# Projecting the third attention's keys straight into the layout of its scores

## The reference, cut to what matters

```python
x = x + _L0_xattn_ref(_layernorm(x), ctx, ...)   # 16 heads of 8, biases, clip
x = x + _L0_ffn_ref(_layernorm(x), ...)          # 8 experts, top 2, gelu
x = x + _L1_xattn_ref(_layernorm(x), ctx, ...)   # 16 heads of 64
x = x + _L1_ffn_ref(_layernorm(x), ...)          # one float8 GEMM, 128 x 128
x = x + _L2_xattn_ref(_layernorm(x), ctx, ctx, ...)  # 16 heads of 8, biases
x = x + _L2_ffn_ref(_layernorm(x), ...)          # 8 experts, relu
x = x + _L3_xattn_ref(...); x = x + _L3_ffn_ref(...)
...
q = (query @ Wq + bq).reshape(B, Nq, 16, 8).transpose(0, 2, 1, 3)   # L2_xattn
k = (key @ Wk + bk).reshape(B, Nk, 16, 8).transpose(0, 2, 1, 3)
v = (value @ Wv + bv).reshape(B, Nk, 16, 8).transpose(0, 2, 1, 3)
attn = softmax(einsum('bhqd,bhkd->bhqk', q, k) * 8 ** -0.5)
return einsum('bhqk,bhkd->bhqd', attn, v).transpose(0, 2, 1, 3).reshape(B, Nq, 128) @ Wo + bo
```

## Time and profile before

| | |
|---|---|
| median of 3 runs | 3913.32 us (3908.84 to 3914.06) |
| the profiled execution, its own time | 3909.72 us |
| its span, first to last instruction | 3908.0 us |
| mean granted TensorE clock | 0.978 |
| PE / ACT / DVE / POOL busy | 93 / 66 / 44 / 12 % |
| DMA, moved | 183.19 MB, mean 47 GB/s |

### The profile page before, as it was taken

One profiled execution on the slowest core, in us unless ns is written; L12 is line 12 of the kernel. 1 busy time (PEld: TensorE's weight loads), 2 busy tenths in 40 slices (PEclk: granted clock), 3 DMA queues, 4 the chain that ended last, 5 costly groups with the idle time before them and its releaser, 6 DMA issues.

```text
span 3908.0 us, 84669 instructions
## 1 busy us (share of the span) xinstructions
PE 3636.0 (93%) x31202; PEld 1368.8 (35%) x31202; DVE 1722.0 (44%) x1678; ACT 2583.1 (66%) x2749; POOL 459.1 (12%) x1842
## 2 busy tenths in 40 slices
PE   7999999999899999999999999968888889897989
PEld 4333333335433333333333333421111123453444
DVE  4222222223377777777777777730000011344344
ACT  5999999983355556555555555469999999401321
POOL 1222222220000000000000000012222222001210
PEclk8999999998999999999999999989999999998989
DMA  5323232212111111111111110050101000000000
GB/s 174 102 76 105 82 100 81 95 70 70 53 32 43 39 38 39 37 39 43 39 37 39 37 37 1 17 149 4 38 4 38 4 29 1 17 27 0 0 13 28
DMA packets 109881, 183.19 MB, mean 47 GB/s; under 512 B 23700, under 2 KB 46896, under 8 KB 107408
## 3 DMA queue, kind: packets, MB, share of 16 engines
q1 hardware_dynamic: 109584, 178.75, 14.9%
HBM read 107.13 MB, written 71.57 MB: 46 GB/s over the span
## 4 chain that ended last, share of the span: by engine, by line
PE 71%; ACT 12%; issue 11%; DVE 4%; ACTq 1%; DMA 0%; SPq 0%; POOL 0%; POOLq 0%; DVEq 0%
PE ps L725 18%; PE ps L750 18%; ACT probs L1050 12%; PE ps L503 7%; PE ps L489 4%; PE ps L437 3%; PE ps L629 3%; PE ps L608 2%; PE ps L866 2%; PE ps L877 2%; PE ps L442 2%; PE ps L925 2%; PE ps L939 1%; PE ps L615 1%; PE ps L262 1%
## 5 line engine op out<-in xcount | busy, mean ns | idle before, releaser
L1050 ACT ACTIVATE probs<-ps 128x1024 f32<-128x1024 f32 x1632 | 1512.8, 1081 | 58.9 <-PE ps L489 58.7
L1149 ACT ACTIVATE probs<-ps 128x1024 f32<-128x1024 f32 x816 | 836.1, 1025 | 596.0 <-PE ps L725 583.1
L1813 DVE TENSOR_TENSOR vbuf<-vbuf,probs 128x1024 f32<-128x1024 f32 (+1 forms) x800 | 972.8, 1224 | 334.7 <-ACT probs L1149 334.7
L503 PE MATMUL ps<-probs,vst 128*32 128x512 f32 x6528 | 863.0, 600 | 118.0 <-ACT probs L1050 117.4
L489 PE MATMUL ps<-qz,kst 32*128 32x512 f32 x3264 | 414.7, 495 | 25.1 <-issue 17.3
L489 PEld LDWEIGHTS ps<-qz,kst 32*128 32x128 f32 x3264 | 162.3, 182 | 710.4 <-issue 682.5
L1302 POOL CAST kst<-kb 128x128 fp32r x816 | 244.8, 300 | 1283.1 <-PE ps L503 1172.5
L1627 DVE COPY qs<-ps 128x512 f32<-128x512 f32 (+1 forms) x208 | 141.7, 681 | 576.0 <-PE ps L437 283.0
L725 PE MATMUL ps<-probs,kb 64*64 64x512 f32 x2560 | 332.2, 589 | 0.0
L725 PE MATMUL ps<-probs,qz 64*64 64x512 f32 x2048 | 269.8, 594 | 7.1 <-issue 6.9
L750 PE MATMUL ps<-probs,qz 64*64 64x512 f32 x2048 | 266.8, 590 | 0.0
(11 more groups left out here) (365 smaller groups left out, 3073.8 us busy)
## 6 DMA issues: line engine op xcount, KB each, us to landing
kv_scratch<-qs SPq DMA_DIRECT2D x192, 256.0 KB, 2.0
kb<-k_scratch SPq DMA_DIRECT2D x24, 816.0 KB, 7.4
kb<-kv_scratch SPq DMA_DIRECT2D x72, 256.0 KB, 2.9
qz<-kv_scratch SPq DMA_DIRECT2D x64, 256.0 KB, 2.9
k_scratch<-klo SPq DMA_DIRECT2D x24, 512.0 KB, 3.5
vbuf<-in_L_ffn_W SPq DMA_DIRECT2D x32, 256.0 KB, 3.1
klo<-kv_scratch SPq DMA_DIRECT2D x32, 256.0 KB, 2.9
qs<-kv_scratch SPq DMA_DIRECT2D x24, 256.0 KB, 2.9
```

The costliest lines, as they stand in the source:

```text
L503: mm = pe.matmul(ps[32 * j:32 * j + 32, 6 + half, :], vst[:, r, 32 * j:32 * j + 32], probs[:, r, j * HT:(j + 1) * HT], start=start, stop=stop)
L1050: act.activation(probs[:, r, b * T:(b + 1) * T].rearrange("p (h n) -> p h n", h=2), ps[:, 2 * buf:2 * buf + 2, :], ACT.Exp, scale=HD8 ** - ...
L1149: act.activation(pr1[:, (u + 2 * odd) % 4], ps[:, 2 * b:2 * b + 2, :], ACT.Exp, scale=HD64 ** -0.5)\
L1813: dve.tensor_tensor(sum1[0:k, odd, h], sum1[0:k, odd, h], e, ALU.add).then_inc(s["added"], 1)
```

## The change

1. **Layer 2's keys never go through DRAM.** `spread_weights` repeats each column of the key weights four times (`w64`) and of the first group's query weights (`wqs`), so a projection lands in the layout of the scores. DVE makes high and low parts with two per-lane factors (`lane`). Chunk 0 of group 0 is made ahead of the attention; the other 12 key chunks, ten of the 13 value chunks and the second half of group 0's queries become 23 jobs (`FIRST2`), done as two half jobs each in tiles 0 to 45 of half 0, all through PSUM bank 7. The keys of the next group are projected in halves 1, 3 and 5, 13 chunks each at `V3_AT`'s tiles, through bank 6. SP loads only queries.
2. **Preparation of layer 2.** Per chunk only a key projection and a square from PSUM remain (`keys2`); the largest norm is taken once per four chunks, each chunk's 128-column blocks lying on four groups of 32 partitions. No sum is taken. The order of PE, ACT and DVE is written out.
3. **Layer 0's norms** also go to four row blocks, with largest value and sum once per four chunks; then a spreading matmul and three small DVE steps pick each head's largest value.
4. **float8:** the layernorm writes bfloat16 directly (the cast goes), and the overflow test masks the sign off where it squared; its four steps (`tensor_tensor`, two `tensor_scalar`, `tensor_tensor`) become three `tensor_scalar`s.
5. `sums1` of the last pair comes after the output projection's first pair; ACT no longer waits for `comb_ready` before `experts8(0)`, and `best` works in another buffer for 8 experts. One small DMA (`bqs`) is added.

```diff
+FIRST2 = [("k", 1), ("k", 2), ("k", 3)]
+FIRST2 += [job for c in range(VEARLY, NC) for job in (("v", c), ("k", c + 1)) if job[1] < NC]
+FIRST2 += [("q", 0)]
...
+                def keys_spread(g, c, p0, p1, bank):
+                    c0, wd = CHUNKS[c]
+                    p1 = min(p1, wd)
+                    for j in range(G):
+                        cut = slice(32 * j, 32 * j + 32)
+                        mm = pe.matmul(ps[cut, bank, p0:p1], w64[:, g, cut], ctxT[:, c0 + p0:c0 + p1], start=True, stop=True)
+                    if p1 == wd:
+                        mm.then_inc(s["k_proj"], 1)
+                def first_job(k, p0, p1):
+                    kind, c = FIRST2[k]
+                    if p0 == 0:
+                        before_kind, before_c = FIRST2[k - 1] if k else ("k", 0)
+                        if before_kind == "k":
+                            pe.wait_ge(s["k_split"], NC + before_c + 1)
+                        else:
+                            pe.wait_ge(s["v_copied"], CHUNKED[2] + before_c + 1)
...
+                            elif gh == 0:
+                                if t < 2 * len(FIRST2):
+                                    first_job(t // 2, t % 2 * (HT // 2), (t % 2 + 1) * (HT // 2))
+                            elif half and g + 1 < NG:
+                                for k in range(V3_PARTS):
+                                    if V3_AT[k] == t:
+                                        next_keys(gh, k // 2, k % 2 * (HT // 2), (k % 2 + 1) * (HT // 2))
...
-            sums1(last_pair, 1, 1)
...
             for p in range(NP):
+                if p == 1:
+                    sums1(last_pair, 1, 1)
...
-            keys8(1, 2, {0: lambda: ln_mean(3), 1: lambda: ln_var(3), 2: lambda: ln_spread(3), 4: float8,
-                         5: lambda: ln_mean(4), 6: lambda: ln_var(4), 7: lambda: ln_spread(4),
-                         9: lambda: queries8(1, 2, 4), 11: lambda: query_norms8(1)})
+            keys2(0)
+            pe.wait_ge(s["x_ready"], 4)
+            ln_mean(3)
+            keys2(1)
+            key_norms(1, 0)
+            ln_var(3)
+            keys2(2)
+            key_norms(1, 1)
+            ln_spread(3)
+            for c in range(3, 9):
+                keys2(c)
+                key_norms(1, c - 1)
+            float8()
...
+            ln_mean(4)
+            keys2(11)
+            key_norms(1, 10)
+            ln_var(4)
+            keys2(12)
+            key_norms(1, 11)
+            ln_spread(4)
+            key_norms(1, 12)
+            pe.matmul(ps[:, 7, :], w64[:, 0, :], ctxT[:, 0:HT], start=True, stop=True).then_inc(s["k_proj"], 1)
+            queries8(1, 4)
+            key_norms_spread(1)
+            pe.matmul(ps[:, 3, :], wqs, z[:, 0, :], start=True, stop=True).then_inc(s["q_proj"], 1)
+            query_norms8(1)
+            values8(1, 2, 0)
+            values8(1, 2, 1)
+            spread_bound2()
+            values8(1, 2, 2)
             attention8(1, 2)
...
-            act.wait_ge(s["comb_ready"], 1)
             experts8(0)
...
+                def next_keys(g, c, bank):
+                    c0, wd = CHUNKS[c]
+                    dve.wait_ge(s["k_proj"], 2 * NC + g * NC + c + 1)
+                    then(dve.tensor_scalar(klo[:, 0, 0:wd].bitcast(F32R), ps[:, bank, 0:wd], lane[:, 1:2], None, ALU.mult))
+                    dve.scalar_tensor_tensor(out=kb[:, g % 2, c0:c0 + wd], in0=ps[:, bank, 0:wd], scalar=lane[:, 0:1],
+                                             in1=klo[:, 0, 0:wd], op0=ALU.mult, op1=ALU.add).then_inc(s["k_split"], 1)
+                def other_queries():
+                    halves = qs[:, :, :].rearrange("p l (h n) -> p l h n", h=2)
+                    dve.wait_ge(s["k_high"], NC + 3)
+                    then(dve.tensor_copy(halves[:, 0].bitcast(F32R), t1))
+                    dve.tensor_tensor(halves[:, 1].bitcast(F32R), t1, halves[:, 0], ALU.subtract).then_inc(s["q_split"], 1)
...
-                then(dve.tensor_tensor(b, a, a, ALU.mult))
-                then(dve.tensor_scalar(b, b, FP8_MAX ** 2, 3e38, ALU.is_gt, ALU.mult))
-                then(dve.tensor_scalar(b, b, 3e38, None, ALU.mult))
-                then(dve.tensor_tensor(b, b, b, ALU.subtract))
+                then(dve.tensor_scalar(b.bitcast(I32), a.bitcast(I32), 0x7FFFFFFF, None, ALU.bitwise_and))
+                then(dve.tensor_scalar(b, b, FP8_MAX, 3e38, ALU.is_gt, ALU.mult))
+                then(dve.tensor_scalar(b, b, 3e38, 0.0, ALU.mult, ALU.mult))
```

More of the change, by code:

```diff
@@ new lines, in key_norms @@
+            def key_norms(n, c):
+                bank, at = norm_place(n, c)
+                pe.wait_ge(s["norm_sq"], n * NC + c + 1)
+                if n == 0 and c and c % 4 == 0:
+                    pe.wait_ge(s["norm_max"], c // 4)
+                for j in range(CHUNKS[c][1] // P):
+                    mm = pe.matmul(ps[32 * j:32 * j + 32, bank, at:at + P], heads[:, :], t3b[:, c % 2, j * P:(j + 1) * P],
+                                   start=True, stop=True)
+                if c % 4 == 3 or c + 1 == NC:
+                    mm.then_inc(s["norm_mm"], 1)
@@ new lines, in key_norms_spread, with values8 @@
+            def key_norms_spread(n):
+                pe.wait_ge(s["norm_max"], n * (KGROUPS + 1) + KGROUPS + 1)
+                pe.matmul(ps[:, 2, 0:P], peak[:, kmax].to_broadcast([P, P]), ident[:, :], start=True, stop=True)\
+                    .then_inc(s["norm_mm"], 1)
+            def values8(n, layer, c):
+                t0, m = VG[c]
+                if c >= 2:
+                    pe.wait_ge(s["v_copied"], CHUNKED[layer] + c - 1)
+                for u in range(m):
+                    mm = pe.matmul(ps[:, 4 + c % 2, u * P:(u + 1) * P], ctxT[:, (t0 + u) * P:(t0 + u + 1) * P],
+                                   w8[:, n, 2, :], start=True, stop=True)
+                mm.then_inc(s["v_proj"], 1)
@@ L393, in keys8 @@
                         .then_inc(s["k_proj"], 1)
-                    t0, m = VG[c]
-                    if c >= 2:
-                        pe.wait_ge(s["v_copied"], CHUNKED[layer] + c - 1)
-                    for u in range(m):
-                        mm = pe.matmul(ps[:, 4 + c % 2, u * P:(u + 1) * P], ctxT[:, (t0 + u) * P:(t0 + u + 1) * P],
-                                       w[:, 2, :], start=True, stop=True)
-                    mm.then_inc(s["v_proj"], 1)
+                    values8(0, 0, c)
@@ L515, in qk_maxima @@
                             return mm
+                        if n and g * 2 + half == 0:
+                            for k in range(len(FIRST2)):
+                                first_job(k, 0, HT)
                         maxima(layer, g * 2 + half, G, 2 * ST, qk_maxima)
@@ L533, in group @@
                             stream(first, lambda t, r: qk(half, t, r), lambda *at: av(g, half, *at), last_sums)
+                            if half and g + 1 < NG:
+                                for c in range(NC):
+                                    next_keys(g * 2 + half, c, 0, HT)
                             if g * 2 + half == CENTRED:
@@ L1248, in _ @@
             diagonal(picks[:, :], [[-1, E16]], 0)
[L1249 removed]
+            for j in range(1, G):
+                diagonal(picks[:, :], [[-1, E16]], -32 * j)
             const(pool.memset(ctxT[C:P, ONES:S], 1.0))
@@ L1648, in without_jobs8 @@
                 def without_jobs8(gi, par, half, p):
+                    if p == 0:
+                        for k in range(len(FIRST2)):
+                            first_job(k)
+                            if k == 0:
+                                other_queries()
+                        dve.wait_ge(s["q_split"], 6)
                     with dve.If(mode >= 1):
```

476 lines of the change are left out of this document (315 added, 161 removed).

## The result

The changed kernel takes 6837.45 us (median of 4 runs, 6832.1 to 6841.72), the kernel before 3911.8 beside it: a ratio of 1.748, 95% interval 1.745 to 1.751. It is 2926 us slower where 22.7 us faster were forecast. Its profiled execution has a span of 6838.0.

The account below looks back on a forecast made before the run. PE's queue was taken as the chain, with ACT's exponentials setting plain tiles and nothing covering layer 2's preparation. Terms -30 + 6.7 + 2.7 - 3.3 + 1.0 + 0.2 = -22.7 gave 3888 us, range 3875 to 3902.

Parts of the forecast that it names:

- fourth layernorm to the register: Layer 2's preparation, from the float8 matmul's result to the bound in the register: 33.9 us becomes 16, gain 17.9, 1.0 given back.
- uncovered jobs: Rival: 124 half jobs in layer 2's halves 0, 1, 3, 5 each add 0.43 us of PE work; 3929 us, chance 0.04.
- PE's wait: Between layer 2's register and PE's first scores: 7.2 us becomes 4.3 with idle DMA engines, gain 2.9, or 0.
- Halves 1 to 6: Layer 2's key jobs in halves 1, 3 and 5 cost 0.90 us each, +2.7 in all; bounds 0 and +8.
- half 7 is the row: Layer 2's old half 7, with 26 half jobs, took 0.90 us over a plain half; taken as price for halves 1, 3, 5.
- Half 0's first tiles: Start of layer 2's half 0: one tile more at half clock adds 0.5 us, within that half's +6.7.
- Layer 0's preparation: Chunks stay paced by stores and loads; a spreading matmul and three small steps ahead of the bound add 1.0; bounds -3, +1.5.
- Layer 1's start: Start of layer 1's attention: `spread_weights` delays DVE some 1.7 us, hidden by the ring of four exponentials; +0.2 us.
- the float8 steps: Layer 2's preparation: one wide step becomes cheaper, one vanishes and the cast goes; gain 2.5 us.
- the output projection: Start of layer 2's preparation: it starts some 3 us earlier and carries the 1.9 us of sums inside; gain 1.4 us.
- the gelu: Layer 0's feed-forward: ACT starts its gelu without waiting for DVE's routing and PE loses its 1.87 wait; gain 3.3, bounds 1.8, 4.
- the hand-over: Layer 2's half 0: PE waits 0.4 us for DVE's two steps behind each of twelve key chunks; 4.8 us, bounds 0 and 17.

## Why the prediction was wrong, and what of it was right

**The step that failed** stands ahead of all terms: the prediction priced "fourth layernorm to the register" and went on with the plain stream, as if the register kept its value. The profile of before shows the register set and the plain stream behind it, but not on what numbers that rests; the code and the diff do. The new norm matmuls write blocks of 32 rows, a chunk of 384 keys fills three of four, and the reduction behind them still reads all 128 rows. None of the rivals had the register turn over. The rival on the slower side, uncovered jobs, had the sign and a price of some 20 us; the mechanism that came costs 2,900. That the register's value is the cause, and the left-over rows what set it, is shown: either put right alone gives 3891 to 3895 us.

**The plain stream's sum.** With the rows mended, 22.7 us forecast stand against 19.5 by the medians and 21.1 by the ratio (15.7 to 26.2). So the forecast holds for the kernel that was meant. The preparation, 65.4 us before from `xT` to the register, took 37.3 to 39.7 in the twelve profiles of changed kernels; the terms made it 39.2.

**Mis-sized terms.** PE's wait, 2.0 for 2.9. Halves 1 to 6, 6.2 for 2.7: the step "half 7 is the row" took a half without a successor for halves that have one. Half 0's first tiles, 1.7 for 0.5. Layer 0's preparation: its register was set 0.1 us later on the mean of twelve profiles, for +1.0. Layer 1's start: "the ring of four exponentials hides" 1.7 us of `spread_weights`, +0.2; it overlooked the reduction of 6.95 us on the same queue, and moving that gave 1.6. Two of the prediction's own signs don't fit its sum: it names "about 101" for half 0, where 96.5 plus its 6.7 is 103.2 and 103.7 was measured; and PE waited 5.2 us behind the register, over the 5 that it called wrong.

**Right:** the float8 steps to 0.1 us, the output projection to 0.2, the third layernorm to 0.1, the gelu's own stretch (3.4 for 3.3), the hand-over (4.4 for 4.8; PE's wait 0.37 for 0.4), the tiles with jobs (1.1 for 1.4), POOL holding PE once in half 0. The step to the register was right to 0.1 in this profile, in part by luck.

## What to carry to other kernels

Before you price an edit, list the data-dependent branches behind it, and ask for each what number decides it and whether the edit changes how that number is made. When a write becomes narrower than the read behind it, the read takes in what an earlier stage left, and it may be harmless in one layer (in layer 0 the same reduction meets old norms) and cost 2,900 us in another. When a row of the trace is used as a price, ask what stands behind it there and here: half 7 has no next group, and the seam was 3.4 us.

## What the runs showed of the hardware

The wait behind a taken branch grew from 5.2 to 7.6 us when six loads of 256 KB ran beside it. A POOL copy of 0.22 us took 1.24 beside one DVE subtraction of two SBUF operands. PE's granted clock was 0.5 through the whole general stream, where PE waits 2.5 us for DVE at each tile of the maxima. And the same stage, layer 0's feed-forward, differed by 6 us between executions with the same edit (158.0 to 164.2), with PE's mean granted clock at 0.98 in the shortest and 0.93 in the longest, more than most of the edits here are worth; terms of a microsecond can be read only in the length of their own stage.
